# Spline coefficients inside the context loop, ternary feed-forwards in tiles of 128 rows, and a first Hadamard butterfly level on TensorE

## What is computed

```python
def quant(x):                                   # per row, 8 bits
    s = max(abs(x)) / qb                        # qb = 127 in layer 0, 128 in layer 1
    return clip(round(x / s), -128, 127) * s
def ternary(w):  return clip(round(w / mean(abs(w))), -1, 1) * mean(abs(w))

# layer 0 feed-forward, weights 512 x 2048 twice and 2048 x 512
h = sigmoid(quant(x) @ ternary(w_gate).T) * (quant(x) @ ternary(w_up).T)
y = quant(h) @ ternary(w_down).T
# layer 1 feed-forward
h = silu(quant(x) @ ternary(w_gate).T) * (quant(x) @ ternary(w_up).T)
y = quant(fwht(h)) @ ternary(w_down).T          # fwht: Walsh-Hadamard over 2048 numbers, / sqrt(2048)
# layer 3 feed-forward: its three weights are Catmull-Rom splines over some 8000 control points each
```

## Time and profile before

| what | value |
|---|---|
| runs | 2653.1 us median of 3 (2650.66 to 2653.58) |
| profiled execution, its own time | 2655.79 us |
| its span, first to last instruction | 2654.0 us |
| PE busy | 2320.2 us (87%) |
| DVE busy | 1250.8 us (47%) |
| ACT busy | 776.7 us (29%) |
| chain that ended last | PE 72%, DVE 18%, ACT 5%, issue 3%, DMA 1% |
| mean granted TensorE clock | 0.952 |

### The profile page before, as it was taken

How to read it: one execution, slowest core, us unless ns; L and a number is a source line. 1 busy time by engine, 2 the same in 40 slices (tenths; PEclk the granted TensorE clock), 3 DMA queues, 4 the chain that set the end, 5 groups by cost and what they waited for, 6 DMA issues and landing times.

```text
span 2654.0 us, 27949 instructions
## 1 busy us (share of the span) xinstructions
PE 2320.2 (87%) x10524; PEld 1358.8 (51%) x10524; DVE 1250.8 (47%) x2497; ACT 776.7 (29%) x1611; POOL 148.7 (6%) x303
## 2 busy tenths in 40 slices
PE   8999999948887869999999986666877788889999
PEld 3555555536554536666666654443433455534444
DVE  1333333562115945555555558974444566621111
ACT  1322333113011323333333324432332455411111
POOL 0000000000000001110001000000000000000000
PEclk9999999979998989999999998887998899989999
DMA  5454433155113010300000030001000211100000
GB/s 200 157 214 159 154 149 122 67 172 211 47 58 159 1 29 19 120 18 24 20 23 24 15 96 17 1 1 31 14 12 7 71 47 47 48 4 4 8 4 12
DMA packets 48042, 171.68 MB, mean 65 GB/s; under 512 B 4561, under 2 KB 24337, under 8 KB 42110
## 3 DMA queue, kind: packets, MB, share of 16 engines
q1 hardware_dynamic: 46182, 132.14, 14.2%
q0 software_dynamic: 1728, 37.75, 3.7%
HBM read 121.58 MB, written 46.47 MB: 63 GB/s over the span
## 4 chain that ended last, share of the span: by engine, by line
PE 72%; DVE 18%; ACT 5%; issue 3%; DMA 1%; SPq 0%; POOL 0%; DVEq 0%; ACTq 0%; POOLq 0%
PE psum L118 61%; PE psum L111 6%; PE psum L1262 4%; DVE R L1098 1%; DVE small L2058 1%; DVE R L1099 1%; ACT WK L2008 1%; DVE small L1101 1%; DVE WK L233 1%; PE psum L1976 1%; DVE WK L1081 1%; DVE small L1085 1%; DVE R L1579 1%; DVE small L1430 1%; ACT R L670 1%
## 5 line engine op out<-in xcount | busy, mean ns | idle before, releaser
L118 PE MATMUL psum<-R,WK 128*125 128x512 f32 (+6 forms) x4000 | 1451.7, 513 | 106.1 <-DVE X L244 40.9
L118 PEld LDWEIGHTS psum<-R,WK 128*112 128x112 f32 (+3 forms) x4000 | 662.6, 176 | 758.1 <-issue 552.6
L111 PE MATMUL psum<-small,WK 112*125 112x112 f32 (+5 forms) x2252 | 309.8, 267 | 132.2 <-DVE WK L233 34.4
L111 PEld LDWEIGHTS psum<-small,WK 112*125 112x125 f32 (+5 forms) x2252 | 249.8, 154 | 241.6 <-issue 130.4
L118 PE MATMUL psum<-WK,R 128*128 128x112 f32 (+4 forms) x1152 | 260.4, 375 | 14.0 <-DVE R L1579 9.0
L118 PEld LDWEIGHTS psum<-WK,R 128*128 128x128 f32 (+2 forms) x1152 | 162.1, 183 | 85.0 <-issue 18.9
L118 PE MATMUL psum<-WK 125*112 125x128 f32 (+5 forms) x1280 | 198.2, 298 | 1.5 <-DVE WK L847 1.2
L118 PEld LDWEIGHTS psum<-WK 125*112 125x112 f32 (+2 forms) x1280 | 162.7, 177 | 66.6 <-issue 49.8
L1430 DVE TENSOR_REDUCE small<-psum 112x1 f32<-112x487 f32 x128 | 85.0, 664 | 221.4 <-PE psum L118 219.5
L1352 ACT ACTIVATE WK<-psum,small 112x487 f32<-112x487 f32 x128 | 96.9, 757 | 259.5 <-DVE small L1432 258.7
L1262 PE MATMUL psum<-R,WK 128*112 128x512 f32 x256 | 120.4, 593 | 0.6 <-ACT WK L1332 0.6
(11 more groups left out here) (208 smaller groups left out, 2088.4 us busy)
## 6 DMA issues: line engine op xcount, KB each, us to landing
R<-in_wf POOLq DMA_DIRECT2D x6, 4096.0 KB, 13.7
d_w<-R POOLq DMA_DIRECT2D x6, 2048.0 KB, 17.9
R<-d_w SPq DMA_DIRECT2D x6, 2048.0 KB, 13.0
WK<-in_ctxT SPq DMA_DIRECT2D x16, 750.0 KB, 5.8
d_v<-WK SPq DMA_DIRECT2D x16, 750.0 KB
R<-in_wq SPq DMA_DIRECT2D x7, 1024.0 KB, 6.9
R<-in_wo SPq DMA_DIRECT2D x6, 1024.0 KB, 16.2
d_k<-X SPq DMA_DIRECT2D x8, 750.0 KB, 3.2
```

Of the source, the lines that this page charges most:

```text
L111: ins = pe.transpose(dst, src, idn[0:k, 0:k])
L118: ins = pe.matmul(dst, lhs, rhs, start=k == 0, stop=k == len(pairs) - 1)
```

## The change

Six edits, in the order of the program:

1. The three tables are all evaluated at the end of batch 6; `powers_of_q` and `coefficients(0)`, then `coefficients(1)` and `(2)`, then the split stand in batch 7 behind the bias sums of s = 0, 1 and 2. The loads of `weights_part` wait only for the products that free their place.
2. Both ternary feed-forwards work on 7 tiles of 128 rows. SP copies rows of x into tiles `xf[i]` as the residual sums of the stage before come (two DMAs a tile), and `back` copies the tiles into `xr` afterwards; `x_ready` of the stages behind wait for those DMAs. Transposes have 128 columns.
3. The scaling of `quantize_h` (1054) moves from DVE to ACT as `scale`: one ACTIVATE over 2048 numbers with a scale and a bias for each row. DVE's order is now: pieces of b1, (ffn0) maximum and `scale_of_h(b1)`, (ffn1) the rounding of b3, then `quantize_x(b0)` and the next statistics, (ffn0) the rounding of b1, (ffn1) butterflies and maximum of b2 and `scale_of_h(b2)`, residual sum of b3. PE's order is as before.
4. ffn1 takes ACT's Silu in place of tanh, the copy 994 and the piece 1074.
5. ffn1's first butterfly level goes: each Hadamard product is 256 columns wide, and two add up in a bank, the second with the matrix and its negative side by side (`plus_minus`). Three levels stay on DVE.
6. In `attention2` unit 8i+4 comes ahead of the `a` products (PE) and the `a` results (DVE), and unit 8i+6 ahead of DVE's residual sum. The rings of the stages share semaphores, with a running base.

```diff
@@ context_part, dve
+                        if b == NB - 1:
+                            if s == 0:
+                                powers_of_q(dve, link)
+                                coefficients(dve, link, 0)
+                            if s == 1:
+                                coefficients(dve, link, 1)
+                                coefficients(dve, link, 2)
+                            if s == 2:
+                                split_coefficients(dve, link)
...
-                        for w in (0, 1) if b == 6 else (2,):
+                    elif b == 6:
+                        dve.wait_ge(sem("spline_inputs"), 16 * 5)
+                        for w in range(3):
@@ weights_part
-                context["filled"](sp)
+                context["raw_free"](sp)
@@ ternary_ffn
+            def sync(sp):
+                if hadamard:
+                    last_values(sp)
+                for i in range(NT):
+                    if i >= 2:
+                        sp.wait_ge(sem(f"{stage}_x{i % 2}"), arrived[i - 2])
+                    for b, of, to in pieces(i):
+                        updates[n - 1].wait_drained(sp, b, "y")
+                        sp.dma_start(xf[i][to, :], xr[of, b, :]).then_inc(sem(f"{stage}_x{i % 2}"), 16)
+            def back(sp):
+                for i in range(NT):
+                    dve_ring.wait_drained(sp, i, "y")
+                    for b, of, to in pieces(i):
+                        sp.dma_start(xr[of, b, :], xf[i][to, :]).then_inc(sem(f"{stage}_back"), 16)
...
-                                for j in range(4):
-                                    ins = product(pe, act_ring.bank[f"w{c}"][0:T, j * P:(j + 1) * P],
-                                                  [(hT[:, 4 * c + j, :], had)])
+                                for j in (0, 2):
+                                    ins = product(pe, act_ring.bank[f"w{c}"][:, j * P:(j + 2) * P],
+                                                  [(hT[:, 4 * c + j, :], had.unsqueeze(1).to_broadcast([P, 2, P])),
+                                                   (hT[:, 4 * c + j + 1, :], plus_minus)])
...
+                def scale(b, src):
+                    act.wait_ge(sem(f"{stage}_down"), b + 1)
+                    if b:
+                        act.wait_ge(sem(f"{stage}_hi"), b)
+                    act.activation(scaled, src, ACT.Identity, bias=magic, scale=rs).then_inc(sem(f"{stage}_scaled"), 1)
...
-                                act.copy(gc[:, c % 2, :], src)
-                            act.activation(th[:, c % 2, :], src, ACT.Tanh, scale=half[:, b1 % 2:b1 % 2 + 1]
-                                           ).then_inc(act_ring.sem_drained, 1)
+                            act.activation(th[:, c % 2, :], src, ACT.Silu if silu else ACT.Tanh,
+                                           scale=half[:, b1 % 2:b1 % 2 + 1]).then_inc(act_ring.sem_drained, 1)
...
+                    if not hadamard and b1 is not None:
+                        scale(b1, h)
                     if b0 is not None:
                         drain_bf16(b0, "xiT", xiT)
+                    if hadamard and b2 is not None:
+                        scale(b2, w1)
...
                         if not hadamard:
                             link(dve.tensor_reduce(hm, hmax, AX, ALU.max))
-                            quantize_h(b1, h)
+                            scale_of_h(b1)
+                    if hadamard and b3 is not None:
+                        quantize_h(b3)
+                    if b0 is not None:
+                        quantize_x(b0)
+                        if b0 + 1 < NT:
+                            stats(b0 + 1)
+                    if not hadamard and b1 is not None:
+                        quantize_h(b1)
...
-                        for k in range(4):
+                        for k in range(1, 4):
@@ attention2, dve (pe alike)
+                    spline["dve"](dve, 8 * i + 4)
                     if b2 is not None:
...
-                    spline["dve"](dve, 8 * i + 4)
                     spline["dve"](dve, 8 * i + 5)
+                    spline["dve"](dve, 8 * i + 6)
                     if b3 is not None:
                         add_to_x(dve, dve_ring, b3)
-                    spline["dve"](dve, 8 * i + 6)
```

More of the change, by code:

```diff
@@ L43, with __init__ @@
 class Ring:
-    def __init__(self, filled, drained, banks, order, tiles=NB):
+    def __init__(self, filled, drained, banks, order, tiles=NB, base=0):
         self.sem_filled, self.sem_drained = filled, drained
@@ L180, in ring @@
             def ring(tag, banks, order):
-                return Ring(sem(f"{stage}_{tag}_filled"), sem(f"{stage}_{tag}_drained"),
-                            [(i, bank[i]) for i in banks], order, tiles)
+                shared = tag if stage not in ("context", "att3b") else f"{stage}_{tag}"
+                r = Ring(sem(f"{shared}_filled"), sem(f"{shared}_drained"), [(i, bank[i]) for i in banks], order, tiles,
+                         rounds.get(shared, 0))
+                rounds[shared] = rounds.get(shared, 0) + len(r.count)
+                return r
             rs = [ring("act", a_banks, a_order), ring("dve", d_banks, d_order)]
@@ L190, in build @@
                            ("wi_stored", 2), ("wscale_stored", 2)] + [(f"coef_stored{i}", 4) for i in range(8)]
+        rounds = {}
         dve_chain, pool_chain = Chain(sem("dve_step")), Chain(sem("pool_step"))
         updates = []
+        TILES = [NB, NT, NB, NT, NB, NB, NB, NT]
         def x_ready(eng, n):
-            if n:
+            if n in (2, 4):
+                eng.wait_ge(sem(f"{'ffn0' if n == 2 else 'ffn1'}_back"), 16 * sum(len(list(pieces(i))) for i in range(NT)))
+            elif n:
                 updates[n - 1].wait_drained(eng, NB - 1, "y")
@@ new lines, in coefficients @@
+            def coefficients(dve, link, w):
+                one, two = ((0, 2), (1, 3), (5, 6))[w]
+                k, a, c = knot[:, w // 2, :], ab[:, w, 0, :], ab[:, w, 1, :]
+                u0, u1, u2, u3 = (part[:, i, :] for i in range(4))
+                for m in range(4):
+                    ins = dve.tensor_scalar(coef[:, one, :, m], cubic[:, w, :, m], STEP ** m, None, ALU.mult)
+                link(dve.tensor_tensor(u0, c, k, ALU.mult))
+                link(dve.tensor_tensor(u1, a, u0, ALU.add))
+                link(dve.scalar_tensor_tensor(u2, u1, 2.0, u0, ALU.mult, ALU.add))
+                link(dve.scalar_tensor_tensor(u3, u0, 2.0, u1, ALU.mult, ALU.add))
+                link(dve.tensor_tensor(u2, u2, k, ALU.mult))
+                link(dve.tensor_tensor(u1, u1, k, ALU.mult))
+                link(dve.tensor_tensor(u1, u1, k, ALU.mult))
+                for m, u in enumerate((u1, u2, u3, c)):
+                    ins = dve.scalar_tensor_tensor(coef[:, two, :, m], u, STEP ** m, coef[:, one, :, m],
+                                                   ALU.mult, ALU.add)
+                link(ins)
+                if w:
+                    side = (4, 7)[w - 1]
+                    dve.tensor_scalar(coef[:, side, :, 0], knot[:, w - 1, :], 1.0 / STEP, None, ALU.mult)
@@ L1108, in pool @@
                 link = pool_chain.on(pool)
[L1109 to L1112 removed]
+                for b in range(NT):
+                    ln_power(pool, link, n, b, P)
+            return dict(load=load, sync=sync, back=back, pe=pe, act=act, dve=dve, pool=pool)
         def attention1(stage, n):
@@ L2251, in _ @@
             stages[0]["sync"](sp, range(2, NB))
-            stages[2]["load"](sp)
+            stages[2]["load"](sp, stages[1]["sync"])
+            stages[1]["back"](sp)
             if upto > 2:
@@ L2259, in _ @@
                     stages[n]["load"](sp)
+            if upto > 3:
+                stages[3]["back"](sp)
             for n in range(4, min(upto, 7)):
```

195 lines of the change are left out of this document (93 added, 102 removed).

## The result

The changed kernel takes 2631.3 us (median of 4 runs, 2628.9 to 2632.4) against 2652.9 us of the kernel before beside it: ratio 0.9919, with a 95% interval of 0.9901 to 0.9936. It is faster, as forecast, but by 22 us and not by 52, and it lies above the upper end of the forecast range (2626). The profiled execution has a span of 2630.6 us, 23.4 less than before.

A forecast was written before the change was run, and what follows sets the result against it. PE held 72% of the chain, DVE 18%; in ffn1 they took turns. Prologue -23, ffn0 +16, ffn1 -31, Silu's table +1.5, attention2 -16 sum to -52.5 on 2655.8: 2603.3, median 2601, range 2570 to 2626.

The forecast's parts named there:

- Prologue, -23 forecast: Prologue: 28.8 us of DVE work move into batch 7 behind PE's products; PE's first attention0 transposes at 594.0, not 617.3.
- ACT's way: Prologue: 16 copies, the later eight behind stores queued on SP; about the same end, or gain only -15 if stores late.
- ffn0, +16 forecast: First ternary feed-forward: `quantize_x` behind the pieces makes a serial turn of 18.2 us; stage 138.7 against 123.1 us.
- rival A: ffn0: the serial chain isn't there, PE gets xi early enough; -15 instead of +16, total 2570; chance 12%.
- The term for the slow clock: ffn0: PE restarts slowly after idling, 1 us added to each 17.3 us turn, so 18.2; bounds 17.3 and 19.
- ffn1, -31 forecast: Second ternary feed-forward: five turns of 25.2 us replace six, 124.7 against 169.9 us; bounds -24 and -36.
- The level on PE is by itself a loss of 1.1 us a turn: ffn1: first butterfly level moved to PE costs 3.5 us there and saves DVE 2.4, both on the cycle.
- Silu's table, +1.5 forecast: ACT: two table switches for ffn1's Silu, between 0 and 2.6 us, half taken; up to 5.3 with drain.
- Rival D: ffn1: ACT's table changes with every function, eight loads a tile; 58 us more, total 2658; chance 4%.
- Attention2, -16 forecast: Attention2: units 8i+4 and 8i+6 put ahead remove PE's waits for `copy_predicated`, 20 us of 31.6; bounds -5 and -20.
- Rival B: Attention2: the stalls only move, since PE's two banks and ACT's copy stay; -3 instead of -16, total 2614; chance 18%.

The follow-up runs named there:

- Run 1: The changed kernel with the first eight coefficient stores issued on SP ahead of attention0's context loads, not behind them: 2618.3 us, ratio 0.9867.
- run 5: The changed kernel with ffn1's first Hadamard level back on DVE (128-column products on PE, four levels on DVE): 2635.1 us, ratio 0.9933.
- Run 7: The changed kernel with attention2's unit 8i+4 behind the a products again on PE, its DVE place kept: 2626.7 us, ratio 0.9902.
- run 4: The changed kernel with ffn0's `quantize_x` one turn ahead on DVE and ACT copying xiT ahead of the scaling: 2598.9 us, ratio 0.98.
- run 8: The changed kernel with ffn1's y on u3's bank, four banks a ring, ACT's scaling later and DVE's rounding behind `quantize_x`: 2603.2 us, ratio 0.9816.
- run 2: The changed kernel with PE making ffn0's y of the older tile before the newest tile's transposes: 2613.0 us, ratio 0.985.

## Why the prediction was wrong, step by step

The direction was right; the sum was 29 us too good, in four terms of which none explains it alone.

- **Prologue, -23 forecast, -7.3 measured.** DVE's dates were right to within 0.6 us: split done at 557.3, the last weight landed at 571.9 (571.5 forecast), quantizing done at 586.9 (586.3). The step that failed is the sentence on ACT's way, "it comes out about the same; if those stores are late, the gain is -15". It named the eight copies that wait for stores, but priced them by no row. SP's queue was followed for the three loads and not for what stands behind them: x and attention0's first context. The trace of the kernel before had the row, 8.28 us for one of these loads, with SP busy until 576.6. There SP then waited for ACT until 596.4, and no issue was late; with PE and ACT 31 us earlier the stores were ready while SP was still at these loads. Run 1 moves eight stores and gives the forecast 594.0.
- **ffn0, +16 forecast, +24.2 measured.** The mechanism was right: the gap ahead of xi is 5.49 us (5.9 forecast), and rival A did not happen. The term for the slow clock, 1 us a turn, was too small. The first y ended at 44.8 us behind the stage's start instead of 40.7 (862.5 less 817.7), the four turns took 77.5 instead of 72.8, and the end as forecast. After each gap the 24 products of y, g0 and u0 took 6.6 to 8.0 us where the prediction, from the earlier trace rows, has 5.3 (3.4 and 1.9): 1.3 to 2.7 us a turn on top of 17.3, which makes 18.6 to 20.0 and so passes the upper bound of 19. The second phase of the start shows the same: its first 8 products took 3.60 us instead of 1.89.
- **ffn1, -31 forecast, -24.5 measured.** The turn was right (25.4 against 25.2). The first turn lost 1.3, the short turn 2.8, the end 1.1, the start 0.9 and the other turns 0.8 (6.9 in all; 0.4 of it the forecast's own rounding). The short turn shows why: its Hadamard products begin at 1765.4, after PE has been idle for 6.2 us, and run at half clock to about 1771. For the clock it had been given 0.6.
- **"The level on PE is by itself a loss of 1.1 us a turn"** was wrong in sign (run 5). The sum of 3.5 less 2.4 took PE's part as the bound on both sides of the edit. The text itself had DVE's other work ending 2 us ahead of PE, and that is how much of the 3.5 can come back while the rest stays as it is.
- **Silu's table, +1.5 forecast, about 0 measured.** Both switches are in the trace, 1.28 us each, and nobody waits for either by the chain. Rival D (a load with each change of function) did not occur. The Trainium skill (ScalarE: Activation LUTs, Table sets: the hidden batching unit) says that cheap functions such as copy and identity are in every set; the trace agrees, with one load for 28 Silu and some 90 copies between them. Of the 2.66 us that the Trainium skill (ScalarE: Activation LUTs, What ACT_TABLE_LOAD costs) gives for a switch, the load's part agrees with the 1.28 us of the rows; no run here shows the drain's part, since ACT waited for other engines behind both loads.
- **Attention2, -16 forecast, -10.0 measured.** Of seven waits of 1.6 to 2.4 us (14.1 in sum) one of 1.7 is left, but seven waits of 0.9 us stand where there had been five, most of them now before unit 8i+4 at its new place; and waits for the residual sum, 1.0 us before, are 2.8. The step that failed first is the reading of the earlier trace rows: the prediction gave "the others, 20 us" to the two moves, but only six waits of 1.6 to 2.4 us, 11.8 in sum, stand in that window. The rest is in waits of 0.3 to 1.0 us that the moves do not touch. The prediction moved this unit in the code and never asked which copy it needs, that of 8i+2, which stands behind `gl` on DVE. Run 7 takes it away again. Rival B (the stalls only move) was thus right in part.
- **Not forecast, -5.8:** attention0's opening 2.8 us shorter, since PE came to it with a clock of 1.00 instead of 0.94 over the first 50 us, and 3.0 in attention1 and behind attention2, which no run here takes apart.

In sum: +15.7, +8.2, +6.5, -1.5, +6.0 and -5.8 make +29.1, against 2630.6 less 2601.5 for the span. What was added up from rows (DVE's dates in the prologue, the gap in ffn0, the turn of ffn1) came out within 1 us. What had no row behind it (ACT's way, the clock after a gap, the copy that a moved unit needs) made the error.

## What to carry to other kernels

When work is pulled forward, follow each in-order queue past the pulled piece: ask what now stands ahead of the first store or load that someone waits for, here x, four loads of 750 KB and two issues of 8.6 and 9.7 us. When DVE and PE take turns, look first for the one order or bank that makes them do so (`quantize_x` behind the pieces in run 4; the bank of y, with two places in the order, in run 8): the same instructions gave 32 and 28 us, each more than the whole change. An edit that trades work between two engines is worth only what the second to finish allows, so price it by the slack on both sides.

## What the hardware showed beyond that

- A gap costs twice. After 5.49 us of idle time PE's granted clock was 0.50 (876.0 to 880.0) and 1.00 again by 882; with gaps of 1.2 us in run 2 some turns still began slowly (8 products in 2.80 us instead of 1.90), and with 0.6 us in run 4 the two turns of the window were at 1.00 throughout. The same products of attention2 took PE 131.0, 133.5 and 137.5 us in three kernels that differ there only in their order, but 133.5 also in the kernel before, which has the order of the 137.5: the order alone doesn't set the clock.
- A DMA issue on SP took 9.0 to 9.7 us when it stood directly behind attention0's four context loads of 750 KB. The third of these loads took 8.57 us in the changed kernel and 8.28 in the kernel before, behind x and two context loads, and 0.6 in run 1, behind small stores. Most other issues here take 0.3 to 0.8 us. In the kernel before, with nothing to issue for 20 us, the first store took 0.33. That the queue has no room behind such loads is an inference; only the durations and the places are shown.
- ACT's scaling of 2048 numbers with a bias and a scale took 2.09 us on 128 rows where 1.93 had been taken from a plain absolute value.
